# A three-stage block on one core: ScalarE's copies of B and C, its logarithm and its group norm in another order, and some steps of the other engines moved

## The chip, the cores and the metric

The kernel runs on one core of a Trainium2 chip. The metric is the time of one execution on the device in microseconds (us), median of three runs. The engines are called PE (TensorE), DVE (VectorE), ACT (ScalarE), POOL (GpSimd) and SP (SyncE, which issues all DMAs here).

## What is computed

Per batch element of eight (64 channels, 32x32 = 1024 positions): a Mamba layer with group norm and a residual, causal attention with 8 heads over the positions, and a mixture of experts that takes the best two of eight. In short:

```python
# Mamba: x is (8, 1024, 64), d_inner 128, d_state 16, dt_rank 4
xh, z = split(x @ W_in)
xh = silu(causal_conv_k2(xh, conv_w, conv_b))
dt_low, Bmat, Cmat = split(xh @ W_x)            # 4, 16, 16
dt = softplus(dt_low @ W_dt + b_dt)
h_t = exp(dt_t * A) * h_{t-1} + dt_t * B_t * x_t   # scan over 1024 steps, 128x16 states
y = (h_t . C_t) + xh * D
x1 = silu(group_norm((y * silu(z)) @ W_out)) + x_in
# attention (per head: d_head 8, causal, softmax), then experts
t = tokens(x1)
t = t + attention(layer_norm(t))
n = layer_norm(t)
p = softmax(n @ router_w + router_b); top_p, top_i = top_k(p, 2); top_p /= sum(top_p)
t = t + sum_k top_p[k] * (n @ expert_w[top_i[k]] + expert_b[top_i[k]])
```

## The kernel before

**Software pipeline.** Each engine has its own program, a Python function `program(a, c, p, b, f)` called for 12 turns. In one turn five batch elements are in work: `a` loads, `c` goes from the convolution through the scan, `p` from the scan's output through the output projection, group norm, residual, first layer norm and q/k projection, `b` through attention, `f` through output projection and experts. Turn 1 has only `c` (and `a`), turn 2 has `c` and `p`, turn 3 adds `b`, turns 4 to 8 have all, turn 9 has `p, b, f`, turn 10 `b, f` and turn 11 `f` alone. A turn has two stages on every engine.

**Stage 1, the score stage.** PE makes scores of q and k in 48 score steps (L1209, causal mask added by L1213), and DVE takes the row maximum of each (L937, `row_maxima`). PE alternates two pairs of banks, so step s waits for the maximum of step s-2. Besides, the tuple `beside` (L941 for DVE, L1218 for PE) says before which score step which work of `c` and `p` is done: on PE `convolution`, `last_folds` (the last four sums over states of `p`, L1137), `gate_projection`, `out_projection`, `dt_before_bias`, `group_mean_product`, `b_product`, `c_product` (all through L1117; B and C share banks 0 and 1, and `c_product` waits until ACT has copied B out), `value_projection` (waits for ACT's copy of C), `x1_to_tokens`, `xn_to_channels`, `qk_projection`; on DVE `gate_scan` (L843), `convolved` (L896, makes xc), `gated` (L930), the group norm's statistics (`channel_statistics` L857 to L862, `group_variance` L869 to L874, `group_scale` L879 to L885), `gate_group_norm` (L890), the layer norm (`centre_first` L901 to L906, `variance` L912, L915) and `qk_less_high` (L924).

ACT in this stage runs one tuple of functions in order (L753): the silu parts (L683, L685), `gate_tanh` (L690), `softplus_start` (L702 to L706: abs, relu, exp), `group_norm` (L694 identity, L696 tanh), `softplus_end` (L710, the logarithm), `take_b` (L730), `high(0)` (L739), `take_c` (L734), and so on. POOL has such a tuple too (L655): `gate_y` (L615), `group_inverse_root` (L619), `add_softplus` (L630, makes dt), `make_u` (L634), `add_residual` (L625, makes x1), `less_high` (L638), `normalise_first` (L608, L516), `less_mid` (L643), `qk_less_mid` (L653). dt and u are each split into three bf16 parts: high is cast by ACT (`high`), POOL takes the rest (`less_high`), ACT casts mid (`mid`, L743), POOL takes low (`less_mid`). SP sends the parts in the fixed order high dt, high u, mid dt, mid u, low dt, low u, four DMAs each (L547), into `dt_rows` and `u_rows`.

**Stage 2, the round stage.** 28 rounds (`ROUNDS`). In each, PE multiplies keys by queries once more (L1313, L1316), adds values (L1328), and spreads dt and u of a number of units to all partitions (L1247; `UNITS_IN[n]` is the number in round n, 32 units in all). ACT makes exp of the scores (L812) and of dt (decay, L773); DVE makes `drive` (L990) of each unit and after every second unit a scan over 1024 steps (L981); POOL multiplies the states by C (L671, `read`). `FOLDS` says in which round PE sums the reads of the first and second quarter (L1137). `TURNS` says in which round which step of `f` stands: transposes, router, experts (PE L1297, DVE L1072 and L1076). `SCALE_AT` is the round in which DVE scales `f`'s second layer norm (L516). All PSUM users of this stage take five banks in a ring, in program order. In round 0, after its units, DVE copies the turned row maxima (L973), which SP sends to DRAM and back into `q_stack` (L569, L572); the first key step (round 4) waits for that.

ACT keeps one set of functions loaded. Tanh and exp of this kernel run in one set, the logarithm (L710) needs another; where the set changes, an `ACT_TABLE_LOAD` stands in ACT's row, at L710 and again before the next function of the other set.

## Time and profile before

| what | us |
|---|---|
| median of 3 runs (1568.96 to 1571.73) | 1569.61 |
| span of the profiled execution | 1566.7 |
| turn 5: first row maximum to first row maximum of turn 6 (600.2 to 770.8) | 170.6 |
| of it the score stage / the round stage | 70.3 / 100.3 |

The profile's rows give an instruction's start in us from the span's start, its duration, engine, line, operation, what it writes and reads and its shape. In brackets stands how long its engine was idle before it and what it then got. The profiled execution's time outside the span isn't recorded; the median of the runs is 2.9 us above the span.

### The profile page before, as it was taken

How to read it: one execution, taken by the hardware profiler on the slowest of the kernel's cores; microseconds unless marked ns; L12 is line 12 of the kernel's file. 1: busy time of each engine (PE TensorE's matmuls, PEld its weight loads, DVE VectorE, ACT ScalarE, POOL GpSimd, SP SyncE). 2: the span in 40 equal slices, each digit the busy share in tenths (PEclk: the TensorE clock that was granted, in tenths of full speed). 3: DMA queues.
4: the chain of work that ended last, by engine and by line, in shares of the span. 5: the costliest groups of instructions: out<-in, count | busy, mean ns of one | idle time of the engine just before them, and what ended most of it. 6: DMA issues, size and time to landing. Idle time of an engine off the chain costs nothing. (4 is left out here: it accounts for less than half of the span.)

```text
span 1566.7 us, 17517 instructions
## 1 busy us (share of the span) xinstructions
PE 1124.4 (72%) x6288; PEld 459.2 (29%) x6388; DVE 1171.5 (75%) x1391; ACT 703.5 (45%) x1298; POOL 512.5 (33%) x272
## 2 busy tenths in 40 slices
PE   1444344778877887679767887778767977796794
PEld 0111111332233333333233332333333323343342
DVE  5198189788678887788788976888778879448445
ACT  0422432337633763366534763366435651470560
POOL 2354544244424432533334432353243331000000
PEclk9666656979987899879987999789986998698995
DMA  1200150020212012111202012201212120111000
GB/s 27 60 1 14 32 111 0 21 70 1 56 41 70 1 32 65 32 45 32 52 20 70 14 24 65 72 1 31 52 25 52 32 52 8 30 32 44 3 14 7
DMA packets 25965, 55.28 MB, mean 35 GB/s; under 512 B 8582, under 2 KB 8970, under 8 KB 23499
## 3 DMA queue, kind: packets, MB, share of 16 engines
q1 hardware_dynamic: 25878, 54.15, 15.2%
q8 instruction: 51, 0.84, 0.2%
q14 instruction: 36, 0.29, 0.1%
...
## 5 line engine op out<-in xcount | busy, mean ns | idle before, releaser
L671 POOL TENSOR_TENSOR read<-state,c_rep 128x1024 f32<-128x1024 f32 x128 | 304.3, 2378 | 458.4 <-DVE state L981 430.9
L937 DVE TENSOR_REDUCE row_max<-ps 128x1 f32<-128x768 f32 (+7 forms) x384 | 349.1, 950 | 95.4 <-PE ps L1213 93.2
L812 ACT ACTIVATE probs<-ps 128x512 f32<-128x512 f32 (+3 forms) x768 | 329.4, 497 | 136.4 <-PE ps L1316 82.9
L981 DVE TENSOR_TENSOR_SCAN state<-decay,drive 128x1024 f32<-128x1024 f32 x128 | 356.6, 2786 | 1.8 <-POOL read L671 1.1
L1209 PE MATMUL ps<-k_stack,q_stack 128*128 128x512 bf16 (+3 forms) x736 | 219.7, 379 | 106.8 <-DVE row_max L937 89.2
L990 DVE TENSOR_TENSOR drive<-ps,b_rep 128x512 f32<-128x512 f32 x256 | 169.5, 676 | 105.0 <-PE ps L1247 102.2
L1313 PE MATMUL ps<-q_stack,k_stack 128*128 128x512 bf16 (+3 forms) x734 | 208.5, 343 | 38.3 <-DVE drive L990 20.0
L773 ACT ACTIVATE decay<-ps,a_scale 128x512 f32<-128x512 f32 x256 | 175.2, 696 | 117.1 <-DVE state L981 101.5
L1328 PE MATMUL ps<-probs,v_aug 128*32 128x512 f32 (+3 forms) x1536 | 169.3, 513 | 5.5 <-ACT probs L812 1.8
L1247 PE MATMUL ps<-dt_rows,pick 128*128 128x512 bf16 x224 | 103.6, 462 | 93.1 <-DVE drive L990 73.8
L1247 PE MATMUL ps<-u_rows,pick 128*128 128x512 bf16 x254 | 116.8, 460 | 47.7 <-DMA u_rows<-read 17.8
L1313 PEld LDWEIGHTS ps<-q_stack,k_stack 128*128 128x128 bf16 x768 | 74.6, 100 | 239.9 <-ACT probs L812 81.8
L1209 PEld LDWEIGHTS ps<-k_stack,q_stack 128*128 128x128 bf16 x768 | 64.5, 104 | 263.5 <-DVE row_max L937 191.7
L1213 PE MATMUL ps<-mask_q,ident_bf 128*128 128x128 bf16 x512 | 120.1, 244 | 11.7 <-DVE row_max L937 11.3
L608 POOL TENSOR_TENSOR ln_s<-ln_s,minus_half 128x8 f32<-128x8 f32 x16 | 26.3, 1643 | 249.3 <-DVE ln_s L915 249.3
L1316 PE MATMUL ps<-mask_k,ident_bf 128*128 128x128 bf16 x512 | 106.6, 229 | 0.4 <-issue 0.3
L1247 PEld LDWEIGHTS ps<-dt_rows,pick 128*128 128x128 bf16 x256 | 27.1, 106 | 164.4 <-DVE drive L990 107.5
L1072 DVE TENSOR_TENSOR moe<-ps,gate_e 128x512 f32<-128x512 f32 x64 | 43.8, 684 | 39.2 <-PE ps L1297 39.1
L1137 PE MATMUL ps<-read,fold 128*32 128x512 f32 x512 | 70.9, 651 | 0.1
L1117 PE MATMUL ps<-xc,w_bc 128*128 128x512 f32 x64 | 47.5, 845 | 30.2 <-ACT b_rep L730 26.0
L1076 DVE TENSOR_REDUCE moe_out<-moe 128x64 f32<-128x512 f32 x64 | 67.4, 1053 | 2.2
L1213 PEld LDWEIGHTS ps<-mask_q,ident_bf 128*128 128x128 bf16 x512 | 56.2, 110 | 42.7 <-issue 20.2
...
## 6 DMA issues: line engine op xcount, KB each, us to landing
...
```

The source lines that it names most:

```text
L671: pool.tensor_tensor(read[:, k % (2 * NG), :], state[:, k % 2, :], c_rep[:, :], ALU.mult)\
L773: act.activation(decay[:, k % 2, halves(h)], bank_of(("dt", k2)), ACT.Exp, scale=a_scale[:, j:j + 1])\
L812: act.activation(probs[:, e % (2 * QUAD), 0:w], bank_of(("scores", e))[:, 0:w], ACT.Exp, scale=SCALE).then_inc(exped.sem, 1)
L937: dve.tensor_reduce(row_max[:, i, h0:h0 + nh], scores[:, :, 0:P * (i + 1)], AX.X, ALU.max, negate=True).then_inc(row_maxed.sem, 1)
L981: dve.tensor_tensor_scan(state[:, k % 2, :], decay[:, k % 2, :], drive[:, k % 3, :], 0.0, ALU.mult, ALU.add).then_inc(scanned.sem, 1)
L990: dve.tensor_tensor(drive[:, k % 3, halves(h)], bank_of(("u", k2)), b_rep[:, halves(h)], ALU.mult)\
L1209: last = pe.matmul(ps[:, bank, 0:w], q_stack[:, h0 + hh, tokens(i)], k_stack[:, h0 + hh, h * BANK:h * BANK + w], start=True, stop=not diag ...
L1213: last = pe.matmul(ps[:, bank, w - P:w], ident_bf[:, :], mask_q[:, :], start=False, stop=True)
L1247: return pe.matmul(bank, pick[:, q, :, :].rearrange("p n e -> p (n e)"), rows[:, g, halves(k2 % 2)], start=True, stop=True)
L1313: last = pe.matmul(bank[:, 0:w], k_stack[:, head, tokens(j)], q_stack[:, head, lo:lo + w], start=True, stop=not diagonal)
L1316: last = pe.matmul(bank[:, 0:P], ident_bf[:, :], mask_k[:, :], start=False, stop=True)
L1328: last = pe.matmul(ps[GW * hq:GW * (hq + 1), ACC, lo:BANK], v_aug[:, j, quad * QUAD + hq, :], probs[:, (QUAD * s + hq) % (2 * QUAD), 0:BAN ...
```

## The change

No instruction of arithmetic is added or taken away. On ACT, B is copied right after softplus's exp; then come the logarithm, then the group norm, then the copy of C, then both high casts. `take_t1` and `take_xn_t` come later among the casts. On POOL `normalise_first` moves behind `less_high(1)`. In the two `beside` tuples and the round tables some numbers change:

```diff
-        UNITS_IN = (2, 2, 2, 1, 0, 2, 2, 0, 2, 1, 2, 1, 1, 1, 2, 1, 0, 0, 1, 1, 2, 1, 1, 2, 0, 1, 0, 1)
-        FOLDS = ((0, 0, 13), (0, 1, 13), (1, 0, 18), (1, 1, 19))
+        UNITS_IN = (3, 1, 2, 1, 0, 2, 2, 0, 2, 1, 2, 1, 1, 1, 2, 1, 0, 0, 1, 1, 2, 1, 2, 1, 0, 1, 0, 1)
+        FOLDS = ((0, 0, 9), (0, 1, 12), (1, 0, 20), (1, 1, 20))
...
-        VARIANCE_AT, SCALE_AT, GATES_AT = 3, 6, 12
+        VARIANCE_AT, SCALE_AT, GATES_AT = 3, 5, 12
```

In `TURNS` the two `xn_t` go from rounds 8 and 9 to 6 and 8, and experts 6 and 7 from round 22 to 23.

```diff
@@ POOL
-                                        (p, add_residual), (c, lambda: less_high(0)), (p, normalise_first),
-                                        (c, lambda: less_high(1)), (c, lambda: less_mid(0)),
-                                        (c, lambda: less_mid(1)), (p, qk_less_mid)):
+                                        (p, add_residual), (c, lambda: less_high(0)), (c, lambda: less_high(1)),
+                                        (p, normalise_first), (c, lambda: less_mid(0)), (c, lambda: less_mid(1)),
+                                        (p, qk_less_mid)):
@@ ACT
-                    for batch, work in ((c, silu_argument), (c, gate_tanh), (c, softplus_start), (p, group_norm),
-                                        (c, softplus_end), (c, take_b), (c, lambda: high(0)), (c, take_c),
-                                        (p, take_t1), (p, take_xn_t), (c, lambda: high(1)), (c, lambda: mid(0)),
-                                        (p, high_qk), (c, lambda: mid(1)), (p, mid_qk)):
+                    for batch, work in ((c, silu_argument), (c, gate_tanh), (c, softplus_start), (c, take_b),
+                                        (c, softplus_end), (p, group_norm), (c, take_c), (c, lambda: high(0)),
+                                        (c, lambda: high(1)), (c, lambda: mid(0)), (p, take_t1), (c, lambda: mid(1)),
+                                        (p, take_xn_t), (p, high_qk), (p, mid_qk)):
@@ DVE, beside
-                        (3, p, gate_scan), (5, c, convolved), (8, c, gated),
-                        (12, p, channel_statistics), (14, p, group_variance), (17, p, group_scale),
+                        (3, p, gate_scan), (6, c, convolved), (8, c, gated), (11, p, channel_statistics),
+                        (15, p, group_variance), (17, p, group_scale), (22, p, gate_group_norm),
@@ PE, beside
-                        ((1, 2), c, convolution), ((1, 2, 2, 3), p, last_folds), ((5, 6), c, gate_projection),
-                        ((9, 10), p, out_projection), ((11, 12), c, dt_before_bias),
-                        ((14,), p, group_mean_product), ((17, 18), c, b_product), ((20, 21), c, c_product),
+                        ((0, 0), c, convolution), ((0, 1, 2, 3), p, last_folds), ((5, 6), c, gate_projection),
+                        ((8, 9), p, out_projection), ((11, 12), c, dt_before_bias), ((14,), p, group_mean_product),
+                        ((17, 17), c, b_product), ((20, 21), c, c_product), ((24,), b, value_projection),
```

ACT in the score stage of a full turn, in program order. The state tile holds softplus's working values, b_rep and c_rep the copies of B and C, read at L694 and L696 the group norm's two halves. Before:

```order
L706 ACTIVATE state<-state 128x1024
L694 ACTIVATE read<-ps,gn_v 64x1024
L696 ACTIVATE read<-ps,gn_v 64x1024
L710 ACT_TABLE_LOAD
L710 ACTIVATE state<-state 128x1024
L730 COPY b_rep<-ps 128x1024
L739 CAST read<-read 128x1024
L734 COPY c_rep<-ps 128x1024
```

Now:

```order
L706 ACTIVATE state<-state 128x1024
L730 COPY b_rep<-ps 128x1024
L710 ACT_TABLE_LOAD
L710 ACTIVATE state<-state 128x1024
L694 ACTIVATE read<-ps,gn_v 64x1024
L696 ACT_TABLE_LOAD
L696 ACTIVATE read<-ps,gn_v 64x1024
L734 COPY c_rep<-ps 128x1024
L739 CAST read<-read 128x1024 x2
```

B's copy stands ahead of the logarithm and the group norm; the group norm's tanh now needs a table load of its own, and the one that stood ahead of the round stage's first decay (L773) is gone.

DVE at the end of the round stage (from expert 5, L1072 and L1076, to the last experts). Before:

```order
L1072 TENSOR_TENSOR moe<-ps,gate_e 128x512
L1076 TENSOR_REDUCE moe_out<-moe 128x64
L990 TENSOR_TENSOR drive<-ps,b_rep 128x512
L981 SCALAR_TENSOR_TENSOR state<-decay,drive 128x1024
L1004 RECIPROCAL den<-ps 128x4x4
L1007 TENSOR_TENSOR attn<-ps,den 128x4x32
L990 TENSOR_TENSOR drive<-ps,b_rep 128x512
L1072 TENSOR_TENSOR moe<-ps,gate_e 128x512
L1076 TENSOR_REDUCE moe_out<-moe 128x64
```

Now:

```order
L1072 TENSOR_TENSOR moe<-ps,gate_e 128x512
L1076 TENSOR_REDUCE moe_out<-moe 128x64
L990 TENSOR_TENSOR drive<-ps,b_rep 128x512
L981 SCALAR_TENSOR_TENSOR state<-decay,drive 128x1024
L1004 RECIPROCAL den<-ps 128x4x4
L1007 TENSOR_TENSOR attn<-ps,den 128x4x32
L990 TENSOR_TENSOR drive<-ps,b_rep 128x512 x2
L981 SCALAR_TENSOR_TENSOR state<-decay,drive 128x1024
L990 TENSOR_TENSOR drive<-ps,b_rep 128x512
L1072 TENSOR_TENSOR moe<-ps,gate_e 128x512
```

Two drives and a scan now stand ahead of expert 6.

DVE at the start of the round stage. Before:

```order
L962 TENSOR_TENSOR max_parts<-max_rest,max_parts 128x8x8
L990 TENSOR_TENSOR drive<-ps,b_rep 128x512 x2
L973 COPY max_t<-ps 24x1024
L990 TENSOR_TENSOR drive<-ps,b_rep 128x512
L981 SCALAR_TENSOR_TENSOR state<-decay,drive 128x1024
```

Now:

```order
L962 TENSOR_TENSOR max_parts<-max_rest,max_parts 128x8x8
L990 TENSOR_TENSOR drive<-ps,b_rep 128x512 x3
L981 SCALAR_TENSOR_TENSOR state<-decay,drive 128x1024
L973 COPY max_t<-ps 24x1024
L990 TENSOR_TENSOR drive<-ps,b_rep 128x512 x2
```

The copy of the row maxima comes behind a third drive and the first scan.

## Rows read from the trace of the kernel before

**Rows 1.** The page, part 1: busy time of each engine in the span.

```profile
PE 1124.4 (72%) x6288; PEld 459.2 (29%) x6388; DVE 1171.5 (75%) x1391; ACT 703.5 (45%) x1298; POOL 512.5 (33%) x272
```

**Rows 2.** Busy time by stretch: score stage, round stage of turn 5; PEclk is granted clock.

```profile
600.20:670.50 70.30, 51.17 (x248) 21.78 (x251) 55.82 (x73) 22.39 (x23) 24.19 (x13) 0.87 0.25 57
670.50:770.80 100.30, 84.09 (x538) 34.07 (x548) 84.35 (x98) 65.29 (x140) 38.59 (x17) 0.92 0.12 27
```

**Rows 3.** DVE in order of time, score stage of turn 5.

```profile
609.33 2.12 DVE L896 SCALAR_TENSOR_TENSOR xc<-drive 128x1024 f32<-128x1024 f32 x1
...
635.22 1.22 DVE L937 TENSOR_REDUCE row_max<-ps 128x1 f32<-128x1024 f32 x1 [5.50 <-PE ps L1213]
```

**Rows 4.** PE in order of time, same stage.

```profile
624.73 1.08 PE L1117 MATMUL ps<-xc,w_bc 128*128 128x512 f32 x2
...
632.23 1.99 PE L1117 MATMUL ps<-xc,w_bc 128*128 128x512 f32 x2 [3.98 <-ACT b_rep L730]
```

**Rows 5.** ACT in order of time, same stage.

```profile
626.61 1.20 ACT L694 ACTIVATE read<-ps,gn_v 64x1024 f32<-64x1024 f32 x1 [4.36 <-DVE gn_v L885]
...
628.92 1.28 ACT L710 ACT_TABLE_LOAD   x1
630.22 1.06 ACT L710 ACTIVATE state<-state 128x1024 f32<-128x1024 f32 x1
631.18 0.99 ACT L730 COPY b_rep<-ps 128x1024 f32<-128x1024 f32 x1
```

**Rows 6.** Who waited for whom in the whole span: us, times, longest.

```profile
PE ps L1117 <- ACT b_rep L730: 26.0, 8, 4.0
```

**Rows 7.** POOL in order of time, score stage of turn 5.

```profile
608.02 2.34 POOL L615 TENSOR_TENSOR state<-state,z_gate 128x1024 f32<-128x1024 f32 x1 [6.73 <-DVE state L843]
...
633.77 2.35 POOL L634 TENSOR_TENSOR read<-read,xc 128x1024 f32<-128x1024 f32 x1
```

**Rows 8.** Lines L890 and L896 over the span: ns, min/median/max, first and last start.

```profile
L890 DVE SCALAR_TENSOR_TENSOR read<-read x8: 1206/1207/1218, 164.1 to 1310.6; 64x1024 f32<-64x1024 f32 x8
...
L896 DVE SCALAR_TENSOR_TENSOR xc<-drive x8: 1224/2122/3397, 37.5 to 1121.4; 128x1024 f32<-128x1024 f32 x8
```

**Rows 9.** DVE in order of time, start of turn 5's round stage.

```profile
673.32 0.67 DVE L973 COPY max_t<-ps 24x1024 bf16<-24x1024 bf16 x1
...
683.38 0.53 DVE L903 TENSOR_SCALAR ln_s<-ln_s 128x8 f32<-128x8 f32 x1
```

**Rows 10.** Turn 1, score stage, all engines in order of time.

```profile
48.79 3.60 PE L1117 MATMUL ps<-xc,w_bc 128*128 128x512 f32 x4 [2.21 <-ACT drive L704]
```

**Rows 11.** SP's issues in order of time: turn 1, then turn 2.

```profile
55.64 2.49 SPq L547 DMA_DIRECT2D dt_rows<-read  x4
...
170.05 2.44 SPq L547 DMA_DIRECT2D dt_rows<-read  x4
184.99 2.41 SPq L547 DMA_DIRECT2D u_rows<-read  x4
...
195.57 2.42 SPq L547 DMA_DIRECT2D u_rows<-read  x4
```

**Rows 12.** DVE, turn 2: the first drive of the round stage.

```profile
200.19 1.47 DVE L990 TENSOR_TENSOR drive<-ps,b_rep 128x512 f32<-128x512 f32 x2 [10.10 <-PE ps L1247]
```

**Rows 13.** DVE in order of time, end of turn 5's round stage.

```profile
740.19 0.69 DVE L1072 TENSOR_TENSOR moe<-ps,gate_e 128x512 f32<-128x512 f32 x1 [2.15 <-PE ps L1297]
...
752.98 0.69 DVE L1072 TENSOR_TENSOR moe<-ps,gate_e 128x512 f32<-128x512 f32 x1 [1.49 <-PE ps L1297]
```

**Rows 14.** PE in order of time, round 19 of turn 5.

```profile
738.03 1.07 PE L1137 MATMUL ps<-read,fold 128*32 128x512 f32 x8
739.03 1.12 PE L1297 MATMUL ps<-w_expert,xn_t 96*128 96x512 f32 x2
```

**Rows 15.** SP, then PE: row maxima into `q_stack`, first key product of turn 5.

```profile
675.71 0.26 SPq L572 DMA_DIRECT2D q_stack<-max_parts_dram  x1
...
680.51 0.63 PE L1313 MATMUL ps<-q_stack,k_stack 128*128 128x512 bf16 x1
```

11 lines of the change are left out of this document (5 added, 6 removed).

## Prediction

> **What bounds the kernel now.** I read the page's busy shares first [rows 1]: DVE is busy for 75% and PE for 72% of the span, so no engine bounds the whole. The busy times by stage [rows 2] say more. In turn 5 the score stage takes 70.3 us with DVE busy for 55.8 and PE for 51.2; the round stage takes 100.3 us with both at 84. Turns 4 to 8 are alike and make up more than half of the span. Then I followed DVE in order of time for a long idle. There is one that stands out: 5.50 us before the row maximum at 635.22 [rows 3]. PE explains it: it stood for 3.98 us at the first product of C (632.23), released by ACT's copy of B [rows 4]. And ACT explains that: B's product was done at about 627.2 (the product of B began at 624.73, its second half about 1.35 us later), but ACT had the group norm from 626.61, then a table load, the logarithm, and only at 631.18 the copy of B [rows 5]. The waits over the whole span show that C waited for B's copy in all 8 turns that have a c [rows 6]. It costs DVE time where scores run beside it: turns 3 to 8, six turns.
>
> **The score stage, part by part.** Nothing is added but places, so each moved step costs its own duration at its new place. I set the new order out from the rows of turn 5, with its times.
>
> *Beginning.* Both halves of the convolution (about 1 us each) now stand ahead of score step 0, with a fold. PE is full there and the sum of its work is unchanged, so the gate of the scan's output (L843) starts within 0.2 us of before. What is gained is a collision: `convolved` (L896) took 2.12 us beside POOL's `gate_y`, which ended at 610.36 [rows 3, 7]; undisturbed it takes 1.22, its shortest of eight [rows 8]. One step later it meets almost no POOL work: -0.7 us net.
>
> *Middle.* `channel_statistics` one step earlier and both halves of B at step 17 let PE run without its 0.4 us wait there. B is ready at about 625.3, and ACT, idle by then, copies it until 626.3. C's product at step 20 is reached by PE at 627.4 and doesn't wait: the 5.50 us shrink to two idles of about 0.4 us. By row maximum 21 DVE would be about 5.5 us ahead. That is the gain at its gross size.
>
> *What is late next.* The group norm. ACT now has: copy of B to 626.3, load 1.28, logarithm 1.06 (to 628.6), identity 1.2, load 1.28, tanh 1.2 [rows 5]: tanh ends at 632.1, and DVE arrives for `gate_group_norm` (L890) at about 631.95. So the second load is just covered; each further us on ACT would cost DVE a us. But POOL makes u (L634, 2.35 us [rows 7]) from 630.95 to 633.3 now, and L890 reads two tiles from SBUF as L896 does. I let it end 1.1 us after POOL, at 634.4: 1.0 us of the gain goes. In the same way the small L903, which took 0.53 instead of 0.17 us beside POOL in one place [rows 9], now falls into `less_high(1)`: 0.7 us more, since that piece of POOL was free before. x1 is then 4.9 us earlier than before, and the layer norm, xn and the q/k products follow it by -4.3. The rest of the stage has the order of before; its small waits stay. Result: **-4.3 us** for each of turns 3 to 8. The bounds: -5.8, if POOL doesn't hold DVE and all idles go; -2.5, if ACT or the residual is a further 1.8 us late.
>
> [...]
>
> [...] In the trace the load took 1.28, and the logarithm started 0.02 us after it. [...]
>
> *Splits.* dt's and u's parts end at about 651 instead of 661.6, so SP's 24 issues are done well ahead of round 0. In full turns this hides: the last u part was awaited 0.5 us while DVE was still at its maxima. Decay 0 starts 1.28 us earlier, without the load; the scan behind it waits for decay 1 and the drives, so it gains nothing there.
>
> **Turn 1** has no scores to hide behind. B's product ends at 52.39 [rows 10], then ACT copies B (1.0), loads (1.28) and takes the logarithm (1.06), to 55.7; before, the logarithm ended at 52.05. SP's 24 issues, back to back from 55.64 [rows 11], all follow from dt. **+3.6 us.**
>
> **Turn 2** has no scores either. Before, high u came only at 184.99, behind xn_t's copy, and SP's last 20 issues ran from there to 198.0; the first drive was at 200.19 [rows 11, 12]. Now both high casts come before the layer norm: dt is 1.5 us later than it was (B's copy and the cold PE ahead of it), but low dt is ready at about 184.8 and low u at 186.9, so SP issues the last four groups' tail from 184.8 to 189.9 and the first drive comes at 192.1. **-8.1 us** (bounds -5 and -10).
>
> **The round stage.** The units' order on PE and ACT doesn't change in rounds 0 and 1. DVE's copy of the maxima moves behind a drive and a scan: from 673.32 [rows 9] to about 676.5. The way through DRAM, whose last DMA was issued at 675.71 and by my estimate landed 2 us later, then ends at about 680.9; the key product is issued at 680.51 [rows 15] and ACT, busy with `f`'s square, takes its result at 685.8. So it costs nothing; without that cover it would cost 3.2 us a turn. The scale of xn at round 5 fills the same hole on DVE as before. The folds of the second quarter leave rounds 18 and 19: the one before expert 4 took 1.07 us on PE and another stood in the round before [rows 14], and DVE waited 2.15 us for expert 4 [rows 13]. That wait goes. PE pays the 2.1 us back in round 20, where DVE has 0.5 us less to spare than it needs. In round 22 a drive and a scan fill DVE's idle of 1.49 us before expert 6 [rows 13]. But the last four rounds go by PE, which idles only when DVE holds a bank; these idles (0.85, 1.37, 0.73, 0.69 us in turn 5) shrink and don't vanish. I take **-1.6 us** for each of turns 4 to 8, bounds -3.5 and +1.5 (folds in the way of the products in rounds 9, 12 and 20, at about 1 us each). Turn 3's rounds, without experts, and turns 9 to 11: 0.
>
> **Sum.** +3.6 - 8.1 - 6 x 4.3 - 5 x 1.6 = -38.3 us. On the span of the profiled execution, 1566.7, that gives 1528.4; the median of the runs lies 2.9 above the span, so 1531.3.
>
> **Rivals.**
>
> *Most of it is eaten (chance 0.17).* The group norm, now behind two loads, becomes the chain: x1 late, then layer norm and q/k late, so a score stage gains 2 us and the rounds nothing. For it: DVE and tanh meet within 0.2 us in my working. 1569.6 + 3.6 - 6 - 12 = about 1555.
>
> *All of it comes (0.20).* No collision at L890, rounds at their lower bound: 1569.6 + 3.6 - 8.1 - 6 x 5.5 - 5 x 3 = about 1517.
>
> *Slower (0.05): TensorE's clock in the round stage.* [...] Two products of 512 columns take 1.99 us at the low level against 1.08 [rows 4]. The low pair comes right behind PE's idle of 3.98 us. If the folds' new places and the waits at the start of the rounds pull it down for longer, a us at the low level costs up to half a us, where PE bounds. It decides from about 13 us more per round stage; at 17 us more in turns 3 to 8 it is +8.5 x 6 = +51 against -38: about 1582. Against it: PE's long idle goes, and PE is denser in a shorter score stage.
>
> *No difference (0.03)*, a mixture of the first and the last. That the change doesn't do what it says is ruled out by the order of the instructions.
>
> **How the numbers follow.** The forecast has 0.55: 1531. Its own spread, from the score stage's bounds, is about 1520 to 1543. The range has to hold 8 in 10; it reaches to 1514 and 1554, and leaves out half of each neighbouring case and the slower one. Faster by over 0.2% (below 1566.5, about what a measurement here can tell): 0.92; within 0.2%: 0.03; slower: 0.05.
>
> **What the new profile should show.** C's product without a wait for the copy of B; L696 with a table load before it, and L773 without one; L890 longer than 2 us in turns 3 to 8; the score stage of turn 5 at about 66 us, the round stage at about 98.7; turn 1's round stage 3.6 us late, and turn 2's first drive at about 195.7 instead of 200.19; moe 4 without its wait. I'm wrong if DVE's idle before row maximum 20 comes back before L890 or L901, or if the first key product waits for the maxima and ACT for it.

## The result, and the profile of the changed kernel

The changed kernel takes 1518.99 us (median of four runs, 1518.73 to 1520.86) against 1569.55 for the kernel before (four runs, 1568.96 to 1571.73): a ratio of 0.9684, interval 0.9672 to 0.9697. The forecast was 1531.3, in a range from 1514 to 1554. So the sign and the range held, and the kernel gained 50.6 us where I had summed up 38.3. The spans of the two traced executions, on which the accounts by stage rest, differ by 49.4 us (1566.7 and 1517.3).

The changed kernel first by busy time of each engine, which answers to [rows 1]:

```profile
PE 1138.1 (75%) x6388; PEld 468.9 (31%) x6388; DVE 1172.0 (77%) x1391; ACT 702.6 (46%) x1298; POOL 512.9 (34%) x272
```

DVE has the same work, 1172 us in both; what went is its idle time. The two stages of turn 5, as in [rows 2]:

```profile
585.40:648.60 63.20, 49.84 (x240) 22.79 (x235) 56.15 (x73) 21.41 (x22) 23.08 (x12) 0.84 0.29 70
648.60:749.50 100.90, 89.20 (x562) 36.08 (x566) 84.32 (x99) 66.67 (x141) 39.75 (x17) 0.90 0.12 26
```

Turn 5 is 164.1 us long instead of 170.6, and it is the longest of its kind: from first row maximum to first row maximum, turns 4, 6, 7 and 8 take 162.4, 163.1, 160.9 and 161.2. The border in these rows is the first row maximum, and it moved: the convolution and a fold now stand ahead of the first score, so some 3 us of the score stage's work lie before the border, and the two lengths can't be held against the forecast's 66 and 98.7 one by one. For the accounts below I divide the program at points that the change doesn't shift: a score stage ends with DVE's first drive (L990), and a round stage with the end of its last scan (L981). Against the kernel before:

| stretch | before, us | change | forecast |
|---|---|---|---|
| up to the first drive of turn 1 | 73.0 | +3.8 | +3.6 |
| score stage of turn 2 | 53.9 | -7.0 | -8.1 |
| score stages of turns 3 to 8, sum | 429.4 | -27.5 | -25.8 |
| round stages of turns 4 to 8, sum | 494.6 | -19.2 | -8.0 |
| all the rest | | +0.5 | 0 |

The changes add up to the 49.4 us of the two spans. So one term is off by far: the round stage gave 3.8 us a turn and not 1.6.

ACT in the score stage of turn 5, in order of time; it answers to [rows 5]:

```profile
607.12 1.01 ACT L730 COPY b_rep<-ps 128x1024 f32<-128x1024 f32 x1 [3.24 <-PE ps L1117]
608.15 1.28 ACT L710 ACT_TABLE_LOAD   x1
609.45 1.06 ACT L710 ACTIVATE state<-state 128x1024 f32<-128x1024 f32 x1
610.41 1.19 ACT L694 ACTIVATE read<-ps,gn_v 64x1024 f32<-64x1024 f32 x1
611.62 1.28 ACT L696 ACT_TABLE_LOAD   x1
612.91 1.20 ACT L696 ACTIVATE read<-ps,gn_v 64x1024 f32<-64x1024 f32 x1
614.01 0.99 ACT L734 COPY c_rep<-ps 128x1024 f32<-128x1024 f32 x1
```

ACT now waits for B's product (3.24 us) and not the other way round; the second load is there. PE's product of C, which stood for 3.98 us in [rows 4], and DVE after it:

```profile
609.24 1.08 PE L1117 MATMUL ps<-xc,w_bc 128*128 128x512 f32 x2
```

```profile
612.25 1.22 DVE L937 TENSOR_REDUCE row_max<-ps 128x1 f32<-128x1024 f32 x1 [0.18 <-PE ps L1213]
614.14 2.29 DVE L890 SCALAR_TENSOR_TENSOR read<-read 64x1024 f32<-64x1024 f32 x1 [0.67 <-ACT read L696]
```

C's product has no bracket, so PE reached it without idling. The row maximum at 612.25 is number 21; number 20 before it, which had 5.50 us of idle in [rows 3], has none worth a row. L890 waits 0.67 us for tanh and then takes 2.29 us instead of 1.21. POOL makes u (L634) from 613.01 to 615.36:

```profile
613.01 2.35 POOL L634 TENSOR_TENSOR read<-read,xc 128x1024 f32<-128x1024 f32 x1
```

Both lines over the span, as in [rows 8]:

```profile
L890 DVE SCALAR_TENSOR_TENSOR read<-read x8: 1206/2286/2290, 175.5 to 1262.7; 64x1024 f32<-64x1024 f32 x8
...
L896 DVE SCALAR_TENSOR_TENSOR xc<-drive x8: 1226/1258/3396, 37.5 to 1080.8; 128x1024 f32<-128x1024 f32 x8
```

In the round stage of turn 5 DVE's experts 4 and 6 (each the first of its pair) answer to [rows 13]:

```profile
715.97 0.69 DVE L1072 TENSOR_TENSOR moe<-ps,gate_e 128x512 f32<-128x512 f32 x1
...
728.39 0.69 DVE L990 TENSOR_TENSOR drive<-ps,b_rep 128x512 f32<-128x512 f32 x1 [1.06 <-PE ps L1246]
...
732.01 0.69 DVE L1072 TENSOR_TENSOR moe<-ps,gate_e 128x512 f32<-128x512 f32 x1
```

Their idles of 2.15 and 1.49 us are gone. In place of the second there is one of 1.06 before a drive.

### The profile page after: what moved, and what is told of

The parts are those of the page before. It is cut to its first block, busy times and chain, and to the rows that moved or that the text cites. A ratio compares the mean times of both kernels' runs of the same rounds, so it can differ in the third digit from the quotient of the medians.

```text
span 1517.3 us, 17622 instructions
## 1 busy us (share of the span) xinstructions
PE 1138.1 (75%) x6388; PEld 468.9 (31%) x6388; DVE 1172.0 (77%) x1391; ACT 702.6 (46%) x1298; POOL 512.9 (34%) x272
## 4 chain that ended last, share of the span: by engine, by line
PE 28%; DVE 25%; issue 14%; ACT 5%; POOL 2%; POOLq 0%; DVEq 0%; ACTq 0%
DVE row_max L937 12%; PE ps L1327 5%; DVE state L981 4%; PE ps L1312 4%; PE ps L1209 3%; PE ps L1246 3%; PE ps L1137 3%; POOL read L671 2%; PE ps L1128 2%; PE ps L1117 2%; DVE drive L990 2%; PE ps L1122 2%; ACT decay L773 1%; ACT probs L812 1%; PE ps L1296 1%
## 5 line engine op out<-in xcount | busy, mean ns | idle before, releaser
L981 DVE TENSOR_TENSOR_SCAN state<-decay,drive 128x1024 f32<-128x1024 f32 x128 | 354.5, 2770 | 1.8 <-POOL read L671 1.1
L1209 PE MATMUL ps<-k_stack,q_stack 128*128 128x512 bf16 (+3 forms) x768 | 230.1, 382 | 94.7 <-DVE row_max L937 91.1
L773 ACT ACTIVATE decay<-ps,a_scale 128x512 f32<-128x512 f32 x256 | 174.9, 696 | 163.8 <-DVE state L981 100.4
L990 DVE TENSOR_TENSOR drive<-ps,b_rep 128x512 f32<-128x512 f32 x256 | 169.7, 677 | 97.0 <-PE ps L1246 96.5
L1312 PE MATMUL ps<-q_stack,k_stack 128*128 128x512 bf16 (+3 forms) x768 | 213.2, 346 | 20.5 <-ACT decay L773 10.8
L1246 PE MATMUL ps<-dt_rows,pick 128*128 128x512 bf16 x256 | 117.3, 458 | 93.5 <-DVE drive L990 70.9
L1137 PE MATMUL ps<-read,fold 128*32 128x512 f32 x512 | 75.0, 676 | 1.4 <-DVE attn L1007 0.9
L1246 PEld LDWEIGHTS ps<-dt_rows,pick 128*128 128x128 bf16 x256 | 26.8, 105 | 155.7 <-DVE drive L990 104.9
L1076 DVE TENSOR_REDUCE moe_out<-moe 128x64 f32<-128x512 f32 x64 | 67.4, 1053 | 2.2
L1296 PE MATMUL ps<-w_expert,xn_t 96*128 96x512 f32 x128 | 66.3, 627 | 0.1
L1072 DVE TENSOR_TENSOR moe<-ps,gate_e 128x512 f32<-128x512 f32 x64 | 43.9, 686 | 27.4 <-PE ps L1296 25.9
```

The lines of the kernel that those rows point to most:

```text
L773: act.activation(decay[:, k % 2, halves(h)], bank_of(("dt", k2)), ACT.Exp, scale=a_scale[:, j:j + 1])\
L981: dve.tensor_tensor_scan(state[:, k % 2, :], decay[:, k % 2, :], drive[:, k % 3, :], 0.0, ALU.mult, ALU.add).then_inc(scanned.sem, 1)
L990: dve.tensor_tensor(drive[:, k % 3, halves(h)], bank_of(("u", k2)), b_rep[:, halves(h)], ALU.mult)\
L1137: last = pe.matmul(ps[GW * g:GW * (g + 1), 2 + h, :], fold[:, q, :], read[:, k % (2 * NG), halves(h)], start=(q == 0), stop=(q == JG - 1))
L1209: last = pe.matmul(ps[:, bank, 0:w], q_stack[:, h0 + hh, tokens(i)], k_stack[:, h0 + hh, h * BANK:h * BANK + w], start=True, stop=not diag ...
L1246: return pe.matmul(bank, pick[:, q, :, :].rearrange("p n e -> p (n e)"), rows[:, g, halves(k2 % 2)], start=True, stop=True)
```

## Experiments

Each experiment takes the kernel before or the changed kernel and moves one group of places; the work is the same in all. "Rounds' tables" are `UNITS_IN`, `FOLDS`, `TURNS` and `SCALE_AT`; "lists" are the two `beside` tuples of DVE and PE. The sums in the text are taken from each kernel's trace, against the kernel before, with the borders of the table above. There is one trace of each kernel, and traces of the same order differ: by up to 3.3 us at the start of turn 1, by up to 2 us in a single score stage, and in the sums too. With the new tables the five round stages gave from 15.2 to 21.7 us in six traces, with the old ones from 0 to 3.1 in five; with all orders of the changed score stage the six score stages gave from 23.4 to 27.5 in four. So a single stretch proves little, and a difference of under some 6 us between two sums proves nothing by itself. The ratios are against runs of the kernel before made beside each group, whose medians lie between 1567.8 and 1570.1 us.

| kernel | us | ratio, interval | score stages 3 to 8 | round stages 4 to 8 |
|---|---|---|---|---|
| changed | 1519.0 | 0.9684, 0.9672 to 0.9697 | -27.5 | -19.2 |
| changed, rounds' tables of before | 1538.2 | 0.9813, 0.9793 to 0.9832 | -25.5 | -0.3 |
| before, rounds' tables new | 1549.3 | 0.9870, 0.9846 to 0.9893 | -1.2 | -19.5 |
| before, ACT's order new | 1561.3 | 0.9946, 0.9931 to 0.9961 | -1.9 | -1.9 |
| before, ACT's and POOL's orders new | 1558.4 | 0.9940, 0.9923 to 0.9957 | -4.5 | -2.1 |
| before, lists new | 1558.4 | 0.9939, 0.9913 to 0.9964 | -8.0 | 0.0 |
| before, ACT's order and lists new | 1543.6 | 0.9845, 0.9808 to 0.9882 | -19.0 | -3.1 |
| changed, start of the stage as before | 1524.6 | 0.9722, 0.9690 to 0.9754 | -16.5 | -21.4 |
| changed, only the folds' rounds new | 1531.6 | 0.9780, 0.9758 to 0.9802 | -23.9 | -9.0 |
| changed, units and experts as before | 1528.2 | 0.9752, 0.9734 to 0.9770 | -23.4 | -10.4 |
| changed, u made after x1 | 1519.4 | 0.9679, 0.9663 to 0.9695 | -25.3 | -21.7 |
| changed, group norm before logarithm | 1526.3 | 0.9730, 0.9697 to 0.9764 | -17.3 | -19.4 |
| changed, three places chosen by turn | 1515.6 | 0.9641, 0.9618 to 0.9664 | -26.8 | -15.2 |

### The two stages apart

The changed kernel with the tables of the rounds as they were, and the kernel before with only these tables new:

```diff
-        FOLDS = ((0, 0, 9), (0, 1, 12), (1, 0, 20), (1, 1, 20))
+        FOLDS = ((0, 0, 13), (0, 1, 13), (1, 0, 18), (1, 1, 19))
```

`UNITS_IN`, `TURNS` and `SCALE_AT` go back likewise, and the second kernel has the same lines the other way round.

> The changed kernel with the round stage's tables (units, folds, turns, scale) as before. Theory: the round stage's gain, 3.9 us in each of turns 4 to 8 by the two traces, is made by the tables, not handed down by the score stage. Then this kernel needs about 1519 + 5 x 3.9 = 1538 us, its turn 5 from first drive to last scan about 99 us again. Rival: the stage starts better because the score stage ends better (parts of dt and u early, no table load, TensorE's clock), and the tables bring only the 1.6 us forecast: about 1527.

> The kernel before with only the round stage's new tables. Theory (tables alone): about 1569.5 - 5 x 3.9 = 1550, the 5.5 us idle of DVE ahead of row maximum 20 unchanged. Rival (the score stage's new end is needed): -1.6 a turn, about 1561.

The two came out at 1538.2 and 1549.3. The tables alone give 19.5 us in the round stages of turns 4 to 8, and without them the changed kernel has nothing there (-0.3). The rest gives 25.5 in the score stages and is nearly absent (-1.2) where only the tables are new. The stages add up within the spread of such traces: neither needs the other. The round stage's 3.8 to 3.9 us a turn are then a matter of the tables alone, and not of splits that come earlier.

### What in the rounds gives 3.8 us instead of 1.6

In the first kernel only the folds' rounds stay new; in the second also those of the turned layer norm and the scale, and what goes back is this:

```diff
+        UNITS_IN = (2, 2, 2, 1, 0, 2, 2, 0, 2, 1, 2, 1, 1, 1, 2, 1, 0, 0, 1, 1, 2, 1, 1, 2, 0, 1, 0, 1)
...
+                 (19, "expert", 4), (20, "expert", 5), (22, "expert", 6), (22, "expert", 7), (26, "out_t", 0),
```

> The kernel after with the units, the turned layer norm, the scale and the experts' rounds of before, and only the folds at their new rounds. Theory (the round stage's gain is the sum of two separate idles of DVE, expert 4's 2.15 us and expert 6's 1.49 us with what follows): the round stage of turns 4 to 8 gives 1.5 to 2.5 us against before, the whole is at 1525 to 1531. Rival (the folds alone give nothing, the idle of expert 4 comes back at expert 6 or in the last four rounds): the round stages give less than 0.7 us and the whole is at 1534 or more.

> The kernel after with the units (of the first two and of rounds 22 and 23) and experts 6 and 7 where they were before; folds, turned layer norm and scale new. Theory (two separate idles, see the run with the folds alone): the round stage of turns 4 to 8 gives 1.7 to 2.7 us against before, so the whole is 5 to 11 us above the changed kernel, 1525 to 1530. Rival (the folds set free what the changed kernel gained, the units only follow): within 2 us of the changed kernel, 1519 to 1521.

They took 1531.6 and 1528.2 us: the first is 0.6 us above the theory's range, the second inside it, and both rivals are out. The folds alone give 1.8 us per round stage of turns 4 to 8 (9.0 in five), folds with the turned layer norm and the scale 2.1, and with the units (of the first two rounds too) and experts 6 and 7 it is 3.8. So there are two gains of about equal size, one at each idle of [rows 13]. DVE in the kernel with the folds alone, experts 4 and 6 and the second-last drive of turn 5:

```profile
716.90 0.69 DVE L1072 TENSOR_TENSOR moe<-ps,gate_e 128x512 f32<-128x512 f32 x1
...
729.77 0.69 DVE L1072 TENSOR_TENSOR moe<-ps,gate_e 128x512 f32<-128x512 f32 x1 [1.49 <-PE ps L1296]
```

```profile
738.68 0.69 DVE L990 TENSOR_TENSOR drive<-ps,b_rep 128x512 f32<-128x512 f32 x1 [1.35 <-PE ps L1246]
```

Expert 4's idle has gone and nothing took its place up to expert 6, whose 1.49 us stand unchanged. In the changed kernel the same two places read 0.15 us at most and none; only the 1.06 us shown above came in. The count for the tail: 1.49 + 1.35 - 1.06 = 1.8 us, which is what the units and experts gave (8.8 us in five turns). DVE's last idle of the stage, 1.63 us before the last drive, is the same in the kernel before, the folds' kernel and the changed one.

### What the score stage needs

The 25 us of the score stages are made of ACT's order, POOL's order and the lists. First ACT's tuple alone in the kernel before (its diff is the ACT part of the change):

> The kernel before with only ACT's tuple in the new order. Theory: the copy of B behind group norm and logarithm is the score stage's stall, so this alone takes most of the 4.3 us in each of turns 3 to 8, pays 3.8 in turn 1, and gains part of turn 2: 1569.5 + 3.8 - 3 - 6 x 3.7 = about 1548. Rival: POOL's order and the steps in the two lists are needed for it, since POOL's second high remainder still stands behind the layer norm and the group norm comes late: about 1560 or more.

It took 1561.3 us, in the rival's range: 0.3 us per score stage. The idle of 5.50 us had gone (row maximum 20 waited 0.19 us here), so where was the gain? PE's two halves of B's product, ACT's copy of B and PE's first half of C's product in turn 5 of that kernel:

```profile
625.81 2.02 PE L1117 MATMUL ps<-xc,w_bc 128*128 128x512 f32 x2
...
628.48 1.77 PE L1117 MATMUL ps<-xc,w_bc 128*128 128x512 f32 x2
631.35 1.13 PE L1117 MATMUL ps<-xc,w_bc 128*128 128x512 f32 x2 [0.23 <-ACT b_rep L730]
```

```profile
630.28 1.01 ACT L730 COPY b_rep<-ps 128x1024 f32<-128x1024 f32 x1 [7.33 <-PE ps L1117]
```

and the same kernel's busy time and granted clock (third number from the end) around B's product:

```profile
623.60:630.40 6.80, 6.06 (x14) 2.34 (x14) 4.72 (x9) 0.12 (x1) 0.55 (x1) 0.54 0.00 0
```

PE was granted 0.54 here. The two halves took 2.02 and 1.77 us, granted 0.50 and 0.61, where [rows 4] have 1.08, granted 1.00. (The granted clock has two values in these traces, 0.50 and 1.00; what lies between is the mean of a stretch. Below they are the low and the full clock.) ACT, with nothing to do for 7.33 us, copied B at 630.28, which counted from the stage's first row maximum is only 1.6 us earlier than before (29.4 against 31.0 us). DVE's idle moved ahead to row maxima 17 and 18 (1.09 and 0.90 us), and L890 had its wait for tanh (1.68 us) and its collision (2.28 us) in full. One turn of this kernel, the seventh, was granted 1.00 there, and the whole product took 2.43 us instead of 4.43: B's copy came at 27.0 us and the stage gained 1.8. So the low clock hides up to 1.8 us of what this order gives, and the rest of the 4.3 us isn't there without the lists.

The low clock doesn't come from ACT's order alone. In the trace with only the tables new, whose score stage is the old one, B's product was granted 0.50 to 0.53 in five of six full stages (4.55 to 4.69 us for the whole product, instead of 2.42 at 1.00), where the kernel before had this in one (4.48 us, granted 0.54). There it cost almost nothing (0.2 to 0.4 us in turns 5 to 8), since ACT came to the copy of B no earlier anyhow.

With POOL's order besides, the lists without either, and lists with ACT's order:

> The kernel before with the new orders of ACT and of POOL, and the places of PE and DVE and the round tables of before. Theory (with PE's product of B as late as before, POOL's order matters little): like ACT's order alone, a score stage of turns 3 to 8 gives 0 to 1 us, the whole is at 1555 to 1562. Rival (ACT's order alone gave nothing because POOL still did the layer norm's product ahead of the second high part, so the parts and the layer norm stood in each other's way): a score stage gives 3 us or more, the whole is at 1545 or less.

> The kernel before with the new steps of PE and DVE in the score stage (both `beside` tuples), and nothing else: ACT, POOL and the round tables of before. Theory (the gain of the score stage needs both: PE's product of B early and ACT's copy of B early): C's product still waits for the copy of B behind group norm and logarithm, a score stage of turns 3 to 8 is within 1.2 us of before, and the whole is at 1562 to 1572. Rival (the steps of PE and DVE were the limit, ACT's order only follows): the score stages give 3 us or more each and the whole is at 1552 or less.

> The kernel before with ACT's new order and the new steps of PE and DVE in the score stage; POOL's order and the round tables of before. ACT alone gave 0.3 us per score stage, the steps alone 1.3, ACT and POOL together 0.75, all three (the changed kernel with the old round tables) about 4.3. Theory (ACT's order and PE's early product of B need each other; POOL's order only matters in turn 2, where it gave 3.6 us): the score stages of turns 3 to 8 give 3.5 to 4.5 us each, turn 2 only 3 to 5 us, and the whole is at 1538 to 1546. Rival (all three need each other, since high u's rest on POOL behind the layer norm holds the q/k path or the parts): the score stages give under 2 us, the whole is at 1553 or more.

ACT and POOL together took 1558.4 us, 0.75 us per score stage: the theory held, and POOL's order isn't what ACT's lacked in the full turns. They gave 7.0 us in turn 2, where ACT alone gave 3.4; POOL's order is worth 3.6 us there, and again 3.6 between the kernel with ACT's order and lists (5.1, below) and the one that adds POOL's order to it, the changed kernel with the tables of before (8.7). By the program's order it is the path from high u to the DMAs, which no scores hide in turn 2.

The lists alone also took 1558.4, and that fits neither expectation. The score stages gave 1.3 us each on average, very unevenly, from 0.8 us lost in turn 3 to 3.2 gained in turn 5. C's product still waited for the copy of B in all eight turns:

```profile
PE ps L1117 <- ACT b_rep L730: 29.0, 8, 4.4
```

The theory's mechanism stood, but its size was off by a few us. What came earlier is the group norm, which in this kernel stands ahead of the copy of B: its statistics and the output projection are one step earlier in the lists. ACT began the identity of turn 5 as soon as DVE had the group norm's values, and copied B behind it and the logarithm:

```profile
623.53 1.20 ACT L694 ACTIVATE read<-ps,gn_v 64x1024 f32<-64x1024 f32 x1 [3.89 <-DVE gn_v L885]
...
628.10 0.99 ACT L730 COPY b_rep<-ps 128x1024 f32<-128x1024 f32 x1
```

Counted from the last scan of the turn before, the copy of B came at 31.1 us instead of 32.3. (From the first row maximum it would be 27.0 instead of 31.0, but 2.8 us of that are the border, which the lists move.) The largest gain, in turn 5, is also the one stage in which C's product was granted 1.00, with 1.12 and 1.08 us for its halves; in the other five they took 1.66 to 2.08, granted 0.50 to 0.65. That isn't the whole of the unevenness: turns 7 and 8 are alike in this and gave 0.05 and 1.9 us.

ACT's order with the lists took 1543.6 us, in the theory's range: 19.0 us in the score stages, 3.2 each. That is more than the sum of the parts (1.9 + 8.0): B's product early and B's copy early need each other, as the theory said. The clock is a part of it, but not all: where B's product was granted 1.00, ACT's order alone gave 1.8 us (turn 7) and the lists alone 0.9 on average (turns 6 to 8), and all orders together 4.3 to 5.2 (turns 5, 7 and 8 of the changed kernel). It is 0.3 us short of the 3.5 that I had named per stage, and this has a cause outside the orders. From turn 4 on, row maxima 12 to 23, L890 and the end of row maximum 47 (62.3 us from the first) are the same as in turn 5 of the changed kernel to within 0.1 us. The difference lies ahead of the first score, in the wait of the first row maximum. In this kernel, and then in the changed one:

```profile
593.03 0.42 DVE L937 TENSOR_REDUCE row_max<-ps 128x2 f32<-128x256 f32 x1 [5.21 <-PE ps L1213]
```

```profile
585.37 0.43 DVE L937 TENSOR_REDUCE row_max<-ps 128x2 f32<-128x256 f32 x1 [3.57 <-PE ps L1213]
```

The changed kernel has both: 3.57 us at turn 5, 5.21 at turn 6. Its windows for the 4.3 us ahead of these two row maxima, and PE's convolution of each:

```profile
581.10:585.40 4.30, 3.43 (x21) 1.20 (x24) 0.70 (x4) 1.36 (x2) 2.35 (x1) 1.00 0.92 177
745.20:749.50 4.30, 4.30 (x19) 0.91 (x22) 0.01 (x1) 1.85 (x2) 0.96 (x1) 0.60 0.95 169
```

```profile
582.05 1.95 PE L1117 MATMUL ps<-xs,w_conv 128*128 128x512 f32 x4 [0.87 <-DVE attn L1007]
```

```profile
744.53 3.08 PE L1117 MATMUL ps<-xs,w_conv 128*128 128x512 f32 x4 [0.87 <-DVE attn L1007]
```

Granted 1.00, the four products took 1.95 us; granted 0.60, 3.08. That is 1.64 us for the stage, and of turns 4 to 8 the low clock fell on the convolution in all five in the kernel with ACT's order and the lists (2.88 to 2.92 us, granted 0.65 or 0.66), on one in the changed kernel, and on one or two in the three traces that differ from the changed kernel in the tables alone (2.89 to 3.15 us, granted 0.60 to 0.65). Why it falls on one turn and not on the next is open.

### The start of the stage

```diff
-                        ((0, 0), c, convolution), ((0, 1, 2, 3), p, last_folds), ((5, 6), c, gate_projection),
+                        ((1, 2), c, convolution), ((1, 2, 2, 3), p, last_folds), ((5, 6), c, gate_projection),
```

DVE's `convolved` goes back to step 5.

> The kernel after with the convolution, the last folds and DVE's xc at their places of before (steps 1 and 2, and 5). Theory (the earlier start only takes xc off POOL's product, 0.85 us of collision): xc takes about 2.1 us again, and a score stage of turns 3 to 8 is 0.5 to 1 us longer than in the changed kernel: 1522 to 1526. Rival 1 (the first row maximum, which waits 5.2 us in the changed kernel behind convolution and fold, is freed, and this is worth more than the collision): faster than the changed kernel, 1513 to 1517. Rival 2 (without the early convolution B's product is late again and the gain of the stage goes): 1530 or more.

It took 1524.6 us, 5.7 above the changed kernel, in the theory's range (the ratios' intervals just overlap, but the fastest run here, 1521.7, is slower than the slowest of the changed kernel, 1520.9). The six score stages are 11.0 us longer than in the changed kernel, which is more than the theory's 0.5 to 1 us each; the round stages and turn 2 happened to be shorter in this trace. Only half of the 11.0 is the theory's collision. xc took 2.12 us again (median of eight), 0.86 more than in the changed kernel. The idles of the first three row maxima sum to the same in both: 0.79 + 1.82 + 2.78 = 5.39 us here, 3.57 + 0.90 + 1.01 = 5.48 in the changed kernel. The other part, in turns 5 to 8, is B's product again: PE was granted 0.60 to 0.62 during the product, which took 3.10 to 3.20 us, and row maximum 17 waited 1.37 us for it in turn 5. In the changed kernel PE is granted 1.00 there in all six turns, and the product takes 1.94 us.

Over all traces, the stages of turns 3 to 8 in which B's product met the low clock (3.10 to 4.69 us for the whole product, granted 0.50 to 0.62; in all other stages it took 1.94 to 2.43, granted 1.00):

| score stage's lists | traces | stages with the low clock at B's product |
|---|---|---|
| as before | before; tables new; ACT's order; ACT's and POOL's orders | 1, 5, 5 and 3 of 6 |
| new, start as before | one | 4 of 6 |
| new | nine | 6 of 54, never more than 1 of 6 |

So with the new lists the low clock rarely falls on B's product. What in them does it isn't shown: the start was put back in one trace only, and in its turns 3 and 4 B's product was granted 1.00 (1.94 us) while the stages were still 1.9 and 2.3 us longer than in the changed kernel.

### DVE and POOL

```diff
-                    for batch, work in ((p, gate_y), (p, group_inverse_root), (c, add_softplus), (c, make_u),
-                                        (p, add_residual), (c, lambda: less_high(0)), (c, lambda: less_high(1)),
+                    for batch, work in ((p, gate_y), (p, group_inverse_root), (c, add_softplus), (p, add_residual),
+                                        (c, make_u), (c, lambda: less_high(0)), (c, lambda: less_high(1)),
```

> The changed kernel with POOL's make_u behind add_residual. Theory: the gating of the group norm (L890) takes 2.29 us in place of 1.21 because POOL makes u beside it; with POOL free there it takes 1.21 and x1 is 1.1 us earlier in turns 2 to 8, while u's parts have some 7 us to spare in full turns: 1519 - 6 x 1.1 = about 1512, less 2 us given back in turn 2, so 1514. Rival: L890 collides with add_softplus or the gain is lost in what follows: 1519.

L890 took 1.22 us, as foreseen, and row maximum 23 ended 1.07 us earlier. Yet the kernel took 1519.4 us, no better than the changed one, which is the rival's time. DVE, then POOL, in turn 5:

```profile
614.37 1.22 DVE L890 SCALAR_TENSOR_TENSOR read<-read 64x1024 f32<-64x1024 f32 x1 [0.67 <-ACT read L696]
...
618.89 0.85 DVE L937 TENSOR_REDUCE row_max<-ps 128x2 f32<-128x256 f32 x2 [1.04 <-PE ps L1213]
...
623.08 1.45 DVE L903 TENSOR_SCALAR ln_s<-ln_s 128x8 f32<-128x8 f32 x1
```

```profile
620.29 4.21 POOL L638 TENSOR_TENSOR decay<-read 128x1024 f32<-128x1024 f32 x2
```

The gain went in two places. At 618.89, row maximum 24, DVE waits 1.04 us for PE, where it waited under 0.2 in turn 5 of the changed kernel. And L903, a step on 128x8 elements that takes 0.17 us alone, takes 1.45: it ends at 624.53, as POOL's rest ends at 624.50. The second would have been enough: in turn 4 row maximum 24 didn't wait, but L903 took 2.19 us, and in all six turns it ended 38.9 us from the first row maximum, as POOL did, against 38.0 in turn 5 of the changed kernel. This is the collision that I had forecast for L903, with a price of up to 2.0 us instead of 0.7.

The other order of logarithm and group norm on ACT, B's copy still ahead of both:

```diff
-                                        (c, softplus_end), (p, group_norm), (c, take_c), (c, lambda: high(0)),
+                                        (p, group_norm), (c, softplus_end), (c, take_c), (c, lambda: high(0)),
```

> The kernel after with ACT's group norm ahead of the logarithm again, B's copy still ahead of both: the second table load inside the score stage goes, and stands ahead of the round stage's first decay instead. Theory (the second load is just covered, and what DVE loses at the residual is POOL's product u beside it): tanh is ready 2 us earlier, DVE's wait of 0.67 us for it goes, the residual runs beside another piece of POOL or none (1.2 to 2.3 us); dt, u and their splits come 2.4 us later, which full turns hide. Score stages of turns 3 to 8 gain 0.5 to 1.5 us more, turn 1 and turn 2 lose up to 2.4 us together: 1512 to 1519. Rival (the late splits come between the layer norm's work on ACT and POOL, and delay xn and q/k): slower than the changed kernel, 1522 to 1530.

1526.3 us: my theory was wrong and the rival's range right (the fastest run here, 1522.2, is slower than the slowest of the changed kernel). The wait for tanh did go. L890 in turn 5, and POOL beside it:

```profile
618.93 2.89 DVE L890 SCALAR_TENSOR_TENSOR read<-read 64x1024 f32<-64x1024 f32 x1
```

```profile
618.40 2.34 POOL L630 TENSOR_TENSOR read<-drive,state 128x1024 f32<-128x1024 f32 x1 [8.57 <-ACT state L710]
620.82 3.21 POOL L634 TENSOR_TENSOR read<-read,xc 128x1024 f32<-128x1024 f32 x1
623.99 2.34 POOL L625 TENSOR_TENSOR read<-read,residual 64x1024 f32<-64x1024 f32 x1
```

L890 began 0.53 us behind POOL's L630, which ended at 620.74, and ended 1.08 us later, at 621.82: 2.89 us instead of 1.21. POOL's L634 in turn began at 620.82 and took 3.21 us instead of 2.35: it ended 2.21 us after L890. Each takes longer beside the other. The rival's reason, the splits, was not the cause, though: what is late here is x1. L625 waits in POOL's queue behind dt and u, and began 1.8 us later in the stage than in the changed kernel (33.0 us from the first row maximum in five of six turns, against 31.1). Row maximum 26 then waited 2.54 us instead of 0.78 for PE, which turns x1. That difference of 1.8 us is about what each stage lost (10.2 us in six). So in the changed kernel the logarithm ahead of the group norm is the better order, in spite of its second table load.

What the two engines share in such a stretch no run shows: the rows show when each ran and how long it took, and for L903 in turn 5 of the kernel with u after x1 that it ended 0.03 us after POOL's rest.

### A version that puts this together

```diff
+                    for batch, work in ((p, gate_y), (p, group_inverse_root), (c, add_softplus), (c and not b, make_u),
+                                        (p, add_residual), (c and b, make_u), (c, lambda: less_high(0)),
+                                        (c and not b, lambda: less_high(1)), (p, normalise_first),
+                                        (c and b, lambda: less_high(1)), (c, lambda: less_mid(0)), (c, lambda: less_mid(1)),
...
+                    for batch, work in ((c, silu_argument), (c, gate_tanh), (c, softplus_start), (c and p, take_b),
+                                        (c, softplus_end), (c and not p, take_b), (p, group_norm), (c, take_c), (c, lambda: high(0)),
```

> The kernel after with three places chosen by turn. In turn 1, where there is no group norm, ACT takes the logarithm before it copies B (as before the change). In turns 3 to 8 POOL makes x1 ahead of u (as in the run with u after the residual), and does the layer norm's product ahead of the second rest (u's), as in the kernel before. Turn 2 keeps the changed kernel's order. Theory (DVE is held by POOL's instruction while both read SBUF, and the run with u after the residual lost at L903 what it won at L890: 1.07 us against 1.28): L890 1.22 and L903 0.17 us, row maximum 24 still waits some 1 us for PE, a score stage of turns 3 to 8 gains 0.5 to 1.2 us on the changed kernel, turn 1 is 2 to 3.5 us shorter: 1509 to 1514. Rival (the rest of the stage goes by PE, which has the value projection and the transposes in a row there, so that DVE waits for PE what it doesn't wait for POOL): only turn 1 gives, 1515.5 to 1517.5. It is at 1519 or more if u's later second part holds ACT's copy of xn_t.

1515.6 us, ratio 0.9641 (0.9618 to 0.9664), against 0.9684 (0.9672 to 0.9697) for the changed kernel: the lowest time of all, above the theory's range and in the rival's. Neither of its two ideas did what I had worked out. The score stages gave nothing on the changed kernel (-26.8 against -27.5), although both collisions had gone; DVE waits for PE instead, as the rival said. This kernel's lines from the second tuple on are one higher (L938 is the row maximum, L891 the residual's product, L904 the small step). DVE, then PE, in the score stage of turn 5:

```profile
611.27 1.22 DVE L891 SCALAR_TENSOR_TENSOR read<-read 64x1024 f32<-64x1024 f32 x1 [0.68 <-ACT read L697]
...
616.10 0.85 DVE L938 TENSOR_REDUCE row_max<-ps 128x2 f32<-128x256 f32 x2 [1.35 <-PE ps L1214]
...
620.29 0.17 DVE L904 TENSOR_SCALAR ln_s<-ln_s 128x8 f32<-128x8 f32 x1
```

```profile
612.18 3.46 PE L1129 MATMUL ps<-w_v,xn_t 96*128 96x64 f32 x16 [0.88 <-ACT c_rep L735]
```

Row maximum 24 waits 1.35 us for scores that stand on PE behind the value projection. Two things make these late. The projection waits 0.88 us for ACT's copy of C, which stands on ACT right behind tanh and so behind both table loads. And it runs for 3.46 us. Turn 4 of the same trace has the same wait for the copy of C, but not the length. Below stand turn 4's projection, and the busy times around both projections, turn 5's first (granted clock third from the end):

```profile
449.47 2.00 PE L1129 MATMUL ps<-w_v,xn_t 96*128 96x64 f32 x16 [0.87 <-ACT c_rep L735]
```

```profile
612.10:615.70 3.60, 3.52 (x19) 3.52 (x20) 2.65 (x3) 0.98 (x2) 3.14 (x2) 0.55 0.16 40
449.40:451.50 2.10, 2.03 (x20) 2.03 (x20) 2.10 (x3) 0.96 (x2) 1.65 (x1) 1.00 0.00 0
```

Granted 0.55 the projection took 3.46 us, granted 1.00 it took 2.00. In turn 4 row maximum 24 didn't wait and came 1.07 us earlier than in turn 4 of the changed kernel: there the whole of L890's gain was kept. In the other five turns it waited 0.77 to 1.42 us beside projections of 2.87 to 3.52 us. The kernel with u after x1 shows the same, turn by turn. So what stands in the way, by these turns, is the value projection at the low clock (granted 0.53 to 0.66 in the five turns), which starts late by the copy of C; the late start alone, granted 1.00, costs DVE nothing. In turn 5 of the changed kernel the projection took 3.29 us too, granted 0.57, and L890's collision lay beside it (row maximum 24 waited 0.11 us), which is why taking the collision away brought nothing in such turns.

In turn 1 the logarithm did come as early as before the change, 2.37 us after the start of softplus's exp (L706). This is ACT in turn 1, this kernel and then the kernel before:

```profile
49.76 1.06 ACT L711 ACTIVATE state<-state 128x1024 f32<-128x1024 f32 x1
50.72 0.99 ACT L731 COPY b_rep<-ps 128x1024 f32<-128x1024 f32 x1
54.73 1.01 ACT L735 COPY c_rep<-ps 128x1024 f32<-128x1024 f32 x1 [3.01 <-PE ps L1118]
55.64 1.99 ACT L740 CAST read<-read 128x1024 bf16<-128x1024 f32 x2
```

```profile
54.51 1.05 ACT L739 CAST read<-read 128x1024 bf16<-128x1024 f32 x1 [1.07 <-POOL read L630]
55.51 1.01 ACT L734 COPY c_rep<-ps 128x1024 f32<-128x1024 f32 x1
```

The high cast of dt, which starts the splits and the DMAs, stands behind the copy of C in the new order, and that waits 3.01 us for PE. So the first drive came 26.73 us after the start of L706, against 24.38 before the change. The kernel with u after x1, whose turn 1 is the changed kernel's, had 26.51 us, the changed kernel itself 28.29; these two differ in PE's product of B alone, which ended 2.15 us after the start of L706 in the one and 3.92 in the other (1.98 us granted 1.00, 3.75 us granted 0.52). Nothing of turn 1's 3 us is thus this version's merit, and where its 3.4 us come from isn't settled; the traced execution, at 1518.9, is the slowest of its five, with 4 us less gained in the round stages than the changed kernel under the same tables, and can't show it. Not tried: the copy of C ahead of the group norm, and behind the high casts in turn 1.

## Why the prediction was right, and where its size was off

**C's product without a wait, the table loads.** Right as forecast: no wait before C's product in the full turns, L696 with a load ahead of it, the first decay (L773) without one (but for turn 1, which has no group norm). The load took 1.28 us and tanh began 0.01 us after it; all 16 loads of the turns (8 at L710, 7 at L696, one at L773) took 1.28 us. The sum with 1.28 for each load gave 4.3 a score stage, and the stages gave 4.6.

**What is late next.** Tanh and DVE did meet: forecast within 0.2 us, measured 0.67 us of wait. L890's collision with POOL was forecast at 1.0 and measured at 1.08: L890 ended at 616.43, 1.07 us after POOL's L634, where I had taken 1.1 from L896, which ended 1.09 us after POOL's `gate_y`. The second half of this step failed: L903 did not collide in the changed kernel (0.17 us), because L890 delays x1 enough to bring it past POOL's work, though by 0.14 us only: POOL's second L638 ended 37.66 us after turn 5's first row maximum, L903 began at 37.80. It is the kernel with u after the residual that has this collision. Gain and loss nearly balance, which is luck: -4.6 us a stage on average over six stages, forecast -4.3, bounds -2.5 and -5.8. Three other traces with the same orders in this stage gave -3.9 to -4.3.

**Beginning of the stage.** L896 went from 2.12 to 1.26 us, forecast -0.7 net. What I didn't see is TensorE's clock during B's product. With the start put back it was low in four of six stages (granted 0.60 to 0.62, 3.10 to 3.20 us instead of 1.94), which is worth about another us in each; that the start decides about it is likely, not shown.

**Turn 1** cost 3.8 (forecast 3.6). Counted from the start of L706 to the first drive it is 28.29 us instead of 24.38. The chain is the one that I had named, by way of dt; the first high cast stands behind the copy of C too, which in the last version came last. About 1.8 us of it hang on the clock during B's product (3.75 us granted 0.52 here, 1.98 us granted 1.00 in the kernel with u after x1), and so the near hit is luck: five other traces with the same order in turn 1 had from +0.9 to +4.3. **Turn 2** gave 7.0 (forecast 8.1, first drive at 195.7). The first drive came at 196.97. B's product took 3.66 us here, granted 0.53; in three traces with the same order it took 1.98 to 2.48, granted 1.00 to 0.77, and turn 2 gave 8.4 to 8.7. Of the "cold PE" of my working the runs show this much: in turn 2 of the kernel before the same product took 3.55 us, granted 0.54. Why it is low there isn't shown. The last term of turn 2's sum was wrong: DVE was not only waiting for the DMAs of u, but stood until 195.61 for the q/k chain:

```profile
195.61 1.22 DVE L924 TENSOR_TENSOR read<-ps,read 128x1024 f32<-128x1024 f32 x1 [10.80 <-ACT read L747]
196.97 1.47 DVE L990 TENSOR_TENSOR drive<-ps,b_rep 128x512 f32<-128x512 f32 x2
```

**The round stage** is the term of the sum that was mis-sized, by 2.2 us a turn or 11.2 in all. Both steps named the right idles. For the folds I wrote that PE pays 2.1 us back in round 20, where DVE has less to spare. It doesn't: with the folds alone the stage gained 1.8 us of 2.15 on average (1.2 to 2.6 by turn). And for expert 6 I wrote that the last four rounds go by PE, so that little would be left; but a DVE idle there went as well (1.35 us before the second-last drive), and only 1.06 us came in for both. Each of the two moves gave about 1.8 us. My value lay within bounds that went from -3.5 to +1.5, and the measured 3.8 is beyond the lower one, as in five of the six traces with these tables: I had priced every move at an engine that isn't full (PE is busy for 84 of 100 us in [rows 2]) as if it were.

**The rest.** The copy of the row maxima came at 653.73 in turn 5, 5.1 us after the first drive; the first key product was issued 10.6 us after that drive, before the change 10.0, and DVE lost nothing by it, as worked out. The 2 us until the last of its DMAs lands were my estimate; the page of the kernel before has 2.0 us from issue to landing for `dt_rows` and `u_rows` and 2.3 and 2.4 for `q_parts_dram` and `k_parts_dram`, and no time for this one. The rival with the clock in the round stage did not come: between first drive and last scan turn 5's was granted 0.91 instead of 0.92 on average, and took 95.1 us instead of 99.0. The clock mattered in the score stage, at single products. What lowers it isn't shown, nor whether idle time of PE does: C's product behind PE's idle of 3.98 us was granted 0.53 (1.99 us for its first half), but behind 0.88 and 0.87 us of idle the value projection was granted 0.55 in one turn and 1.00 in the other.

Of the cases, "all of it comes" (1517) has the nearest time, but only half of its reason held: the rounds went beyond their bound (its sum has 3 us for them, where the bound was 3.5), while L890's collision was there. The likeliest case had the score stage right and the rounds wrong.
